# Four stacked attention layers: the queries' stack moved by groups of four heads, and a new order on TensorE

## What is computed

```python
q, k, v = heads(x @ qkv_w + qkv_b)                 # each (12, 256, 16)
attn = einsum('bqd,bkd->bqk', q * scale, k)
rel_h = einsum('bhwc,hkc->bhwk', q_as_grid, Rh)    # query row against key row
rel_w = einsum('bhwc,wkc->bhwk', q_as_grid, Rw)    # query column against key column
attn = softmax(attn + rel_h[..., :, None] + rel_w[..., None, :])
out = (attn @ v) @ proj_w + proj_b
x = x + out                                        # x was group-normed ahead of q, k, v
```

## Time and profile before

| | us |
|---|---|
| median of three runs | 183.39 |
| lowest, highest of them | 183.13, 187.79 |
| the profiled execution's own time | 184.84 |
| its span, first to last instruction | 183.0 |

### The profile page before, as it was taken

How to read it: one execution, slowest core, us unless ns; L and a number is a source line. 1 busy time by engine, 2 the same in 40 slices (tenths; PEclk the granted TensorE clock), 3 DMA queues, 4 the chain that set the end, 5 groups by cost and what they waited for, 6 DMA issues and landing times.

```text
span 183.0 us, 2753 instructions
## 1 busy us (share of the span) xinstructions
PE 165.6 (90%) x1017; PEld 107.3 (59%) x1027; DVE 87.9 (48%) x223; ACT 69.8 (38%) x157; POOL 35.2 (19%) x61
## 2 busy tenths in 40 slices
PE   7799938999979989999998998998999899999992
PEld 2478606665534657755446765766665578466551
DVE  2453715773455487665451014375335342277561
ACT  4152300675113231784036622345641042227820
POOL 7932068407930035005000000000000000000000
PEclk9999996999999996999999999999999999999999
DMA  4999966991370044000000000630000036600001
GB/s 123 268 251 185 235 174 170 272 308 24 14 173 2 4 129 129 0 0 4 0 0 0 0 0 4 172 86 2 0 4 0 0 79 182 172 0 4 0 2 43
DMA packets 11421, 14.70 MB, mean 80 GB/s; under 512 B 3312, under 2 KB 8816, under 8 KB 11392
## 3 DMA queue, kind: packets, MB, share of 16 engines
q1 hardware_dynamic: 7712, 12.08, 26.9%
q0 software_dynamic: 3248, 2.05, 6.7%
q10 hardware_dynamic: 448, 0.39, 0.7%
HBM read 7.96 MB, written 0.20 MB: 45 GB/s over the span
## 4 chain that ended last, share of the span: by engine, by line
PE 74%; DVE 9%; ACT 6%; DMA 5%; issue 3%; SPq 1%; ACTq 0%; POOL 0%; DVEq 0%; POOLq 0%
PE PC L920 11%; PE RING L798 9%; PE RING L894 9%; PE PB L931 6%; PE RING L853 5%; DMA QS<-RL 4%; PE RING L1101 3%; PE PA L1107 3%; PE RING L1016 2%; PE PB L816 2%; PE PB L798 2%; PE PB L853 2%; PE PA L990 2%; PE PC L831 2%; ACT QS L528 2%
## 5 line engine op out<-in xcount | busy, mean ns | idle before, releaser
L798 PE MATMUL RING<-WARM 128*128 128x512 bf16 x127 | 35.1, 409 | 2.1 <-POOL WARM L344 1.3
L536 ACT ACTIVATE PR<-RING 128x512 f32<-128x512 f32 (+1 forms) x48 | 25.3, 555 | 9.1 <-PE RING L894 8.9
L920 PE MATMUL PC<-PR,VX 128*32 128x256 f32 (+1 forms) x192 | 23.3, 367 | 0.0
L721 DVE TENSOR_REDUCE NM<-RING 128x2 fp32r<-128x512 f32 (+1 forms) x32 | 19.9, 652 | 5.7 <-PE RING L853 5.5
L798 PEld LDWEIGHTS RING<-WARM 128*128 128x128 bf16 x135 | 12.8, 104 | 15.0 <-issue 2.4
L894 PE MATMUL RING<-QS,KS 128*128 128x256 f32 (+1 forms) x96 | 20.2, 309 | 1.0 <-ACT QS L528 0.8
L894 PEld LDWEIGHTS RING<-QS,KS 128*128 128x128 f32 x96 | 14.1, 191 | 9.8 <-issue 6.3
L721 DVE TENSOR_REDUCE NM<-PB 128x2 fp32r<-128x512 f32 (+1 forms) x16 | 10.5, 657 | 14.6 <-PE PB L853 14.5
L920 PEld LDWEIGHTS PC<-PR,VX 128*32 128x32 f32 x192 | 9.6, 109 | 8.3 <-ACT PR L536 1.3
L728 DVE STREAM_TRANSPOSE TURNED_U<-PC 128x256 f32<-128x256 f32 x12 | 5.4, 450 | 15.8 <-PE PC L920 15.8
L528 ACT ACTIVATE QS<-PA 4x512 fp32r<-4x512 f32 x20 | 11.1, 576 | 4.5 <-PE PA L869 4.4
(11 more groups left out here) (163 smaller groups left out, 251.4 us busy)
## 6 DMA issues: line engine op xcount, KB each, us to landing
WQKV<-in_w SPq DMA_DIRECT2D x2, 576.0 KB, 7.5
WO<-in_wo SPq DMA_DIRECT2D x4, 288.0 KB, 9.4
QS<-QHL SPq DMA_DIRECT2D x6, 192.0 KB, 6.2
W<-in_ff SPq DMA_DIRECT2D x2, 576.0 KB, 7.7
WQKV<-in_w SPq DMA_DIRECT2D x2, 432.0 KB, 6.9
KS<-in_hot POOLq DMA_DIRECT2D x4, 192.0 KB, 9.5
KS<-KH SPq DMA_DIRECT2D x4, 192.0 KB, 6.0
QS<-RH SPq DMA_DIRECT2D x4, 192.0 KB, 4.6
```

Source lines behind the costliest of these rows:

```text
L536: A(PR[:, h % NPR, 0:n], exponents(l, h)[:, 0:n], ACT.Exp).then_inc(sem("probs"), 1)
L721: V.tensor_reduce(NM[1 if h < EARLY else g % 2][:, :, h % GH], MAXIMA[h % 3][:, 0:2 * n_keys].rearrange("p (q k) -> p q k", q=2), AX.X, AL ...
L798: M(bank, WARM[:, 0:P], WARM[:, :], start=True, stop=True)
L920: ins = M(columns(h)[:, reach(l, k)], VX[:, k, h, :], half(PR[:, h % NPR, :], l, k), start=(k == 0 and l != 2), stop=(k == 1), skip_group_ ...
```

## The change

1. **Moves.** In layers 0 and 3 each of the seven moves into `QS` is cut into three, one for each group of four heads. The weights' order (`order2`) changes so that a group g of `QHL` holds the heads 4g to 4g + 3. "q stack" now counts the seven moves of group 0; the new semaphores "second heads" and "third heads" count seven each. SP's order: high parts of group 0 (two), low part of group 0, high of group 1 (two), the three moves of keys, high of group 2 (two), low of groups 1 and 2, then the relative terms, group by group, w = 0 ahead of w = 1 in each. With three moves of keys these are 24 issues instead of 10. A high part moves as soon as its own group is ready.
2. **Waits.** The loop starts on "q stack" and "k stack"; `for_maxima(4)` waits for "second heads" and `for_maxima(8)` for "third heads". The weights that layer 0 loads afterwards wait for the third heads.
3. **PE ahead of the loop** (layers 0 and 3): `relative` w = 0, two dummies, values' chunk 0, `relative` w = 1, two dummies, values' chunk 1. That is two dummies more. "v psum" is signalled at the last.
4. **Dummies.** `DMA_WARM` goes from (16, 0, 0, 20) to (18, 3, 0, 8).
5. **Loop** (all layers): the dummy behind `for_maxima(6)` goes, and `for_maxima` 7, 8 and 9 each stand one place earlier; `turn_maxima(1)` stands ahead of `values(0)`; `turn_maxima(2)` ahead of `scores(6)`.

```diff
-DMA_WARM = (16, 0, 0, 20)
+DMA_WARM = (18, 3, 0, 8)
...
-                if l in REL_LAYERS:
+                def move_group(signal, block, src, g, count):
+                    move(signal, rows_of(queries, block)[:, g * GH:(g + 1) * GH], src[:, g, :],
+                         ("q stack", "second heads", "third heads")[g], count)
+                def high_queries(g):
                     for block in (Q_AGAIN, Q_HIGH):
-                        move("qh", rows_of(queries, block), QHL[0:64, :, :], "q stack")
+                        move_group("qh", block, QHL[0:64], g, g + 1)
+                def low_queries(g):
+                    move_group("ql", Q_LOW, QHL[64:128], g, g + 1)
+                high_queries(0)
+                low_queries(0)
+                high_queries(1)
                 for block in (Q_HIGH, Q_LOW):
                     move("kh", rows_of(KS, block, KEY0, REG1), KH[:, :, :], "k stack")
-                if l in REL_LAYERS:
-                    move("ql", rows_of(queries, Q_LOW), QHL[64:128, :, :], "q stack")
                 move("kl", rows_of(KS, Q_AGAIN, KEY0, REG1), KL[:, :, :], "k stack")
-                if l in REL_LAYERS:
+                high_queries(2)
+                low_queries(1)
+                low_queries(2)
+                for g in range(NG):
                     for w in range(2):
                         for name, block, src in (("rel h", ROW_HIGH, RH), ("rel l", ROW_LOW, RL)):
-                            move(name, rows_of(queries, block + w), src[64 * w:64 * w + 64, :, :], "rel stack", 2 * w + 2)
+                            move_group(name, block + w, src[64 * w:64 * w + 64], g, 2 * w + 2)
...
+                if h in (GH, 2 * GH) and l in REL_LAYERS:
+                    pe.wait_ge(*upto("second heads" if h == GH else "third heads", l, 7 * 16))
...
                 for c in range(2):
-                    for k in range(NC):
-                        M(s[:, c * C:(c + 1) * C], XN[:, k, c * P:(c + 1) * P],
...
-                ins.then_inc(sem("v psum"), 1)
-                if l in REL_LAYERS:
-                    keep_warm(RINGS[0][1][:, :], 2)
-                    relative(l)
+                    if l in REL_LAYERS:
+                        relative(l, c)
+                        keep_warm(RINGS[0][1][:, :], 2)
+                    value_chunk(l, c)
...
                 for_maxima(l, 6)
-                keep_warm(PC[1][:, :], 1)
+                for_maxima(l, 7)
                 if l == 2:
                     reg_scores(l, 0)
                 scores(l, 2)
-                for_maxima(l, 7)
+                for_maxima(l, 8)
                 scores(l, 3)
-                for_maxima(l, 8)
+                for_maxima(l, 9)
+                turn_maxima(l, 1)
                 values(l, 0)
-                turn_maxima(l, 1)
-                for_maxima(l, 9)
                 for_maxima(l, 10)
...
                 values(l, 2)
+                turn_maxima(l, 2)
                 scores(l, 6)
-                turn_maxima(l, 2)
...
-    order2 = np.arange(C).reshape(GH, NG, HD).transpose(1, 2, 0).reshape(NG, 64)
+    order2 = np.arange(C).reshape(NG, GH, HD).transpose(0, 2, 1).reshape(NG, 64)
```

More of the change, by code:

```diff
@@ L262, in build @@
                     "qh": {0: NG, 1: NC, 2: NC, 3: NG}, "ql": {0: NG, 1: NC, 2: NC, 3: NG},
-                    "q stack": {l: 3 * 16 for l in range(LAYERS)}, "later heads": {l: 6 * 16 for l in (1, 2)}}
+                    "q stack": {l: (7 if l in REL_LAYERS else 3) * 16 for l in range(LAYERS)}, "later heads": {l: 6 * 16 for l in (1, 2)}}
         signals |= {"x": {l: 3 * NC if l == 1 else NC for l in range(LAYERS)}, "sums": {0: 1}}
         signals |= {name: {l: count for l in REL_LAYERS} for name, count in {
-            "rel psum": 4, "rel h": 4, "rel l": 4,
-            "rel stack": 4 * 16}.items()}
+            "rel psum": 4, "rel h": 4, "rel l": 4, "second heads": 7 * 16, "third heads": 7 * 16}.items()}
         signals |= {name: {t: count for t in (1, 3)} for name, count in {
@@ L318, in _ @@
                     continue
[L319 removed]
+                def move_group(signal, block, src, g, count):
+                    move(signal, rows_of(queries, block)[:, g * GH:(g + 1) * GH], src[:, g, :],
+                         ("q stack", "second heads", "third heads")[g], count)
+                def high_queries(g):
                     for block in (Q_AGAIN, Q_HIGH):
[L321 removed]
+                        move_group("qh", block, QHL[0:64], g, g + 1)
[4 more added lines that the diff above has]
+                high_queries(1)
                 for block in (Q_HIGH, Q_LOW):
                     move("kh", rows_of(KS, block, KEY0, REG1), KH[:, :, :], "k stack")
[L324 to L325 removed]
                 move("kl", rows_of(KS, Q_AGAIN, KEY0, REG1), KL[:, :, :], "k stack")
[L327 removed]
+                high_queries(2)
+                low_queries(1)
+                low_queries(2)
+                for g in range(NG):
                     for w in range(2):
                         for name, block, src in (("rel h", ROW_HIGH, RH), ("rel l", ROW_LOW, RL)):
[L331 removed]
+                            move_group(name, block + w, src[64 * w:64 * w + 64], g, 2 * w + 2)
                 if l == 0:
[L334 removed]
+                    sync.wait_ge(*upto("third heads", 0, 7 * 16))
                     load(later_loads)
@@ L817, in project, with relative, value_chunk @@
                 return ins
[L819 to L834, removed]
+            def relative(l, w):
+                if w == 0:
+                    pe.wait_ge(sem("rel lo"), 1)
+                    pe.wait_ge(*upto("ql", l, NG))
+                else:
+                    take("w", l, 0)
+                table = 2 * REL_LAYERS.index(l) + w
+                for i in range(SIDE):
+                    terms = rel_bank(l, w, i // 8)[0:64, i % 8 * NG * SIDE:(i % 8 + 1) * NG * SIDE]
+                    queries = QHL[:, :, i * SIDE:(i + 1) * SIDE] if w == 0 else QHL[:, :, i:T:SIDE]
+                    for part in (RELH, RELL):
+                        lhsT = part[:, table, (SIDE - 1 - i) * GH:(NREL - i) * GH]
+                        ins = M(terms.rearrange("p (g c) -> p g c", g=NG), lhsT, queries, start=(part is RELH),
+                                stop=(part is RELL))
+                    if i % 8 == 7:
+                        ins.then_inc(sem("rel psum"), 1)
+            def value_chunk(l, c):
+                s = RINGS[0][0][:, c * C:(c + 1) * C]
+                for k in range(NC):
+                    M(s, XN[:, k, c * P:(c + 1) * P], WQKV[l][:, k, key_column(l) + C:key_column(l) + 2 * C], start=(k == 0),
+                      stop=False)
+                ins = M(s, ONES[:, :], VB[0:1, l, :], start=False, stop=True)
+                if c:
+                    ins.then_inc(sem("v psum"), 1)
             def for_maxima(l, h):
```

5 lines of the change are left out of this document (removed).

## The result

| | before | after |
|---|---|---|
| median of the runs, us | 183.52 | 178.64 |
| lowest, highest | 183.13, 187.79 | 177.62, 178.91 |
| the profiled execution's own time | 184.84 | 178.91 |
| its span | 183.0 | 177.1 |

The ratio of after to before is 0.9723, with a 95% interval of 0.9678 to 0.9767. That is 4.9 us less on the medians, and 5.93 less between the two profiled executions. The prediction was 175.7, its range 173.9 to 179.8: the time lies inside, 2.9 above the point.

The account below looks back on a forecast made before the run. PE (74%) was taken to bound the kernel, leaving its idle time, dummies and low clock to win. 2.25 + 1.1 + 1.0 + 1.75 - 0.15 + 0.7 + 1.0 = 7.65 less gave 177.2 profiled, 175.7 median; range 173.9 to 179.8.

Parts of the forecast that it names:

- Layer 0's start: Start of layer 0's loop: fewer bytes ahead of the last needed move, start at 26.0 for 28.27, 2.25 us less.
- Layer 0's clock: Behind layer 0's loop start: with idle time 0.5 instead of 4 the clock stays up, 1.1 us less.
- Layer 1's start: Start of layer 1's loop: three dummies take idle time and keep the clock, 1.0 us less.
- Layer 3's start: Start of layer 3's loop: SP's queue, not the data, is last; start at 158.8 for 160.53, 1.75 us less.
- The new wait at `for_maxima(4)`: Layer 3's loop: PE waits 0.3 for the second heads, half of it hidden, 0.15 us more.
- The loops of layers 0, 1 and 3: `for_maxima(7)` moves into the wait for ACT's copy: 0.24 us less each, 0.7 in three layers.
- rival D: The loop's new order does not pay; PE waits for DVE at the turn: 0.3 x 3 lost, 0.7 missing, 177.3; chance 0.10.
- Layer 2: Layer 2's loop: ACT's copies end before PE wants them at `reg_scores(1)`, 1.0 us less.
- From the profile to the median: Median 1.45 lower than the profiled execution; the same 7.65 taken off it gives 175.7.
- A: Clock falls all the same in layer 0 or layer 1: 176.8 with one, 177.9 with both; chance 0.25.
- B: Layer 0's moves bound by one slow engine or their number: start at 28, clock falls, 178.8; chance 0.20.
- C: Issues limit layer 0: at 1.68 each the sixteenth lands at 37.5, time 188.3; decides at 1.4; chance 0.05.

Follow-up runs that it names:

- moves_whole: Kernel after with the seven moves of twelve heads whole again (ten issues per layer, order and waits of before): ratio 0.9899, 3.2 us slower than the kernel after.
- part3_only: Kernel before with part 3 of the change (the order on PE ahead of the loop) alone: ratio 1.0091, 1.7 us slower than the kernel before.
- loop_only: Kernel before with part 5 of the change (the loop's order, all four layers) alone: ratio 0.9886, 2.1 us less than the kernel before.
- warm1_only: Kernel before with layer 1's three dummies alone (`DMA_WARM[1]` = 3): ratio 1.0001 to the kernel before, no difference.
- warm1_back: Kernel after with layer 1's three dummies out (`DMA_WARM[1]` = 0): ratio 0.9765 to the kernel before.
- loop_back: Kernel after with part 5 undone (the loop's order of before): ratio 0.9841 to the kernel before, 2.1 us more than the kernel after.
- sp_order: Kernel after with SP's issues reordered so the last move the loop's start needs is 13th, not 16th: ratio 0.9818 to the kernel before, slower than the kernel after.
- part3_back: Kernel after with part 3 undone exactly (order of before on PE ahead of the loop, two dummies): ratio 0.9745 to the kernel before.

## Why the prediction was right, and where it was off

Against the profiled execution's 184.84 the sum said 7.65 less; between the profiles it was 5.93. The steps:

- **Layer 0's start: 2.25 predicted, 1.71 measured.** Landing at 26.5 for 25.8. The last needed RL was issued at 22.89, not at 21.5: four moves of QHL took 4.75 where I had 2.5, and I had allowed only for KL's and RL's stall. The mechanism, fewer bytes ahead of the last move, held (`moves_whole`); that the size is right to 0.5 is worth little, since the start differs by 1.5 between executions of the same code (26.56, 26.81, 25.27).
- **Layer 0's clock: 1.1 and 1.08.** The price was right, in part by luck: it was the middle of 0.5 and 1.7. In all three profiles that stood idle for 3.1 to 4.2 ahead of this loop (before, `part3_only`, `moves_whole`) the clock fell behind the start, and in the eleven that stood idle for 2.22 or less it did not. But that the fall belongs to the idle time was too simple: in `loop_only` and `warm1_only` it had fallen ahead of the loop (0.73 and 0.59 between 18 and 22), and the loop kept its clock behind a wait for the same last move.
- **Layer 1's start: 1.0 and 0.81.** The clock stayed, but `for_maxima(6)` then waited 0.56 for the last KL; I had not asked what comes last once PE is faster there. That the dummies keep the clock fits the profiles (none of ten against three of four), but no run shows the gain in time to be theirs: `warm1_only` gained nothing, and `warm1_back` took as long in layer 1 as the kernel after.
- **Layer 3's start: 1.75 and 0.76, the term most off.** The sixteenth issue went out 10.46 behind the first, not 9.45: one KH cost 1.10, and four moves of QHL 2.90 with the gap of 0.44 among them. Landing behind the issue took 2.0, for 1.9 taken. By the fit in the Trainium skill (DMA: Bandwidth & Descriptors, Anatomy of one DMA), made on DMAs that GpSimd issued, an estimate for 64 KB would be 2.15, 0.15 more than layer 3 shows. The advice to coalesce in the Trainium skill (DMA: Bandwidth & Descriptors, Rules for kernel authors) was the better guide in layer 3, where whole moves start the loop 0.5 sooner, and the worse one in layer 0, where they start it 3.15 later.
- **The new wait at `for_maxima(4)`: 0.3 and 0.33**, with an effect of 0.27 instead of 0.15.
- **The loops of layers 0, 1 and 3: 0.7 and 1.0** (0.48, 0.06, 0.47), not 0.24 each. The 0.24 is the `for_maxima(7)` that left this stretch; where the other 0.2 of layers 0 and 3 comes from is not shown. The turn did not wait for DVE there, and did in layer 1, for 0.30: rival D's mechanism came in one layer, its 1.6 us did not. That the sum is near is in part luck. Layer 2: 1.0 and 0.85.
- **From the profile to the median.** I took the same 7.65 off both. The profiled execution of before was 1.45 above the median that I took (183.39), that of after only 0.27 above its own; of the 2.9 us by which the point was missed, 1.7 is the steps above and 1.2 this. The mean clock does not explain it: executions of the kernel before with 0.977 to 0.979, where the profiled one lies, took 181.96 to 184.92. What does is open, and so a gain read off one execution is not the gain of the median.

Rivals: A, a fall all the same, did not come in the four executions of the kernel after (0.998 to 1.000), but the kernels nearest to it have it (`loop_back` 0.981 to 0.999, `warm1_back` 0.981 to 1.000). B, one slow engine, did not come: the landing moved by 1.5. C, issues as the limit in layer 0, was wrong in its price (0.6 to 1.8 us per issue, not always 1.68), but its stalls were there and put the sixteenth issue 1.4 later than I had it. That the queue and not the data sets layer 3 was in the prediction itself, and held. Two slips in the prediction's sums bear on nothing: B with A is 179.9 where the range says 179.8, and C would decide at 1.35 us per issue (10.2 + 15 x 1.35 + 2.1 = 32.6), not at 1.4.

## What to carry over

Cutting moves pays where bytes are waited for, and costs one issue each where the queue is waited for; count the issues up to the last one that the consumer needs, and also up to the last of all, since an earlier start (`sp_order`) turned that into a worse wait later. Two parts with a second issuing engine, in layers 1 and 2 too, gave the lowest time here; what each of the two is worth was not separated. Where the limiting engine has a dummy or a wait, put real work of a later step there that is already possible, as the loop's order did: 2.1 us with nothing else changed. But moving a step earlier also makes it meet waits that it did not meet before, as the turn did in layer 1.

## What was not expected of the hardware

- A move from SBUF to SBUF costs SP 0.55 to 0.7 us whatever its size (64, 96, 128 or 192 KB). But in layer 0, with the loads in flight, single ones took up to 2.2 (`part3_back`), and in layer 3 up to 1.3 (a KH in `sp_order`).
- The granted clock falls in different places in executions of almost the same program. In `warm1_only` it fell at 18.7, while PE did the relative terms and had been busy for 3.84 of the 4 us from 14 to 18. A fall ahead of the wait for the DMA was hidden by that wait in `warm1_only` (start at 27.95, for 28.27 in the profile of before, where it did not fall there); one under the dummies of `part3_back` lengthened them from 4.04 to 6.90 and moved the start.
- With whole moves and relative terms that were ready sooner, layer 0's transfers ran slower (169 GB/s in `part3_only` and 191 in `moves_whole`, for 208) and ended later; the cause is open.
